# Value-matrix rows of 272 columns, 288 floats apart, with six zero router columns; two tiles of x loaded later

## The reference

```python
# x (4, 1024, 256), ctx (4, 77, 256), side (4, 16), 16 heads of 64
q = LN2(LN(x)) @ Wq;  k, v = split(LN1(ctx) @ Wkv)
q = q * (1 + side) + side                        # per batch and head
attn = softmax(q @ k.T * 64 ** -0.5)             # per head, over 77 rows
x = x + concat_heads(attn @ v) @ Wout
# experts on y = LN(x)
logits = y @ Wr                                  # 9 experts
w, idx = top_k(softmax(logits), 2);  w = w / w.sum()
x = x + sum_e w_e * ((silu(y @ Wg[e]) * (y @ Wu[e])) @ Wd[e])   # 256 -> 704 -> 256
```

## Time and profile before

| | us |
|---|---|
| median of 3 runs (lowest, highest) | 809.7 (808.88, 810.03) |
| profiled execution, its own time | 810.75 |
| its span, first to last instruction | 809.0 |
| TensorE busy | 781.2 |
| VectorE busy | 662.2 |
| ScalarE busy | 622.3 |
| GpSimd busy | 386.2 |

### The profile page before, as it was taken

How to read it: one execution, slowest core, us unless ns; L and a number is a source line. 1 busy time by engine, 2 the same in 40 slices (tenths; PEclk the granted TensorE clock), 3 DMA queues, 4 the chain that set the end, 5 groups by cost and what they waited for, 6 DMA issues and landing times.

```text
span 809.0 us, 19727 instructions
## 1 busy us (share of the span) xinstructions
PE 781.2 (97%) x6011; PEld 744.7 (92%) x6011; DVE 662.2 (82%) x1614; ACT 622.3 (77%) x1967; POOL 386.2 (48%) x539
## 2 busy tenths in 40 slices
PE   7998999999999999998999999999999999999994
PEld 7766999999999999897999999999999999999994
DVE  7787798898888887888688988788887878879782
ACT  5878898899899888844677877777787877778772
POOL 3321587688678766771324343332434333233343
PEclk9999999999999999998999999999999999999998
DMA  8375710410410020635475373465656556483222
GB/s 278 116 187 163 224 35 34 144 41 27 148 38 28 34 86 28 212 115 172 102 216 141 51 218 87 104 151 141 182 151 163 146 144 164 90 224 79 47 26 28
DMA packets 78212, 96.40 MB, mean 119 GB/s; under 512 B 10723, under 2 KB 65435, under 8 KB 77979
## 3 DMA queue, kind: packets, MB, share of 16 engines
q1 hardware_dynamic: 64667, 77.25, 31.2%
q0 software_dynamic: 13440, 17.90, 12.6%
HBM read 109.45 MB, written 30.23 MB: 173 GB/s over the span
## 4 chain that ended last, share of the span: by engine, by line
PE 88%; DVE 4%; ACT 2%; issue 2%; POOL 1%; DVEq 1%; DMA 0%; SPq 0%; POOLq 0%; ACTq 0%
PE banks L355 25%; PE banks L356 25%; PE banks L357 25%; PE banks L1471 4%; PE banks L1637 2%; PE banks L1451 2%; PE banks L1485 2%; DVEq L1690 1%; PE banks L1422 1%; PE banks L1434 1%; ACT wq_head L1071 1%; PE banks L1355 1%; ACT prob L1138 1%; PE banks L1609 0%; DVE hid_f L2128 0%
## 5 line engine op out<-in xcount | busy, mean ns | idle before, releaser
L355 PE MATMUL banks<-tok_t_hi,wgt_hi 128*128 128x256 f32 x704 | 201.5, 286 | 3.7 <-issue 2.8
L1015 POOL DMA_INDIRECT result<-res,tok_id x72 | 123.9, 1721 | 164.1 <-ACT res L1273 144.7
L357 PE MATMUL banks<-tok_t_hi,wgt_lo 128*128 128x256 f32 x704 | 197.1, 280 | 0.0
L356 PE MATMUL banks<-tok_t_lo,wgt_hi 128*128 128x256 f32 x704 | 197.0, 280 | 0.0
L1138 ACT ACTIVATE prob<-banks,row_min 128x77 f32<-128x77 f32 x512 | 161.5, 374 | 2.3 <-DVE row_min L1840 2.3
L355 PEld LDWEIGHTS banks<-tok_t_hi,wgt_hi 128*128 128x128 f32 x704 | 133.6, 190 | 5.9 <-issue 5.8
L356 PEld LDWEIGHTS banks<-tok_t_lo,wgt_hi 128*128 128x128 f32 x704 | 133.2, 189 | 0.0
L357 PEld LDWEIGHTS banks<-tok_t_hi,wgt_lo 128*128 128x128 f32 x704 | 133.1, 189 | 0.0
L1138 ACT ACTIVATION_READ_ACCUMULATOR prob<-banks,row_min 128x1 f32 x512 | 130.6, 257 | 0.0
L355 PE MATMUL banks<-wgt_hi,hid_hi 128*128 128x256 f32 x360 | 101.2, 281 | 0.7 <-DVE hid_hi L2156 0.7
L356 PE MATMUL banks<-wgt_lo,hid_hi 128*128 128x256 f32 x360 | 100.8, 280 | 0.0
(11 more groups left out here) (273 smaller groups left out, 2208.6 us busy)
## 6 DMA issues: line engine op xcount, KB each, us to landing
wgt<-in_L_ffn_Wg SPq DMA_DIRECT2D x29, 704.0 KB
wgt<-in_L_ffn_Wu SPq DMA_DIRECT2D x29, 640.0 KB
wgt<-in_L_ffn_Wd SPq DMA_DIRECT2D x29, 640.0 KB
tok<-expert_in SPq DMA_DIRECT2D x32, 258.0 KB, 3.8
spare_wgt<-in_L_ffn_Wg SPq DMA_DIRECT2D x9, 704.0 KB, 4.5
spare_wgt<-in_L_ffn_Wu SPq DMA_DIRECT2D x9, 640.0 KB, 6.1
spare_wgt<-in_L_ffn_Wd SPq DMA_DIRECT2D x9, 640.0 KB, 5.7
valmat_f<-valmat_dram SPq DMA_DIRECT2D x4, 1197.0 KB, 6.3
```

Of the source, the lines that this page charges most:

```text
L355: nc.tensor.matmul(to, a[0], b[0], start=first, stop=False)
L356: nc.tensor.matmul(to, a[0], b[1], start=False, stop=False)
L357: return nc.tensor.matmul(to, a[1], b[0], start=False, stop=last)
L1015: nc.gpsimd.indirect_dma_start(out, bass.IndirectOffsetOnAxis(ap=tok_id[:, t % NOTES, a:a + 1], axis=0), res[i][:, a, :], None, compute_op ...
```

## The change

A value row has DE = 272 columns, the next multiple of 16 after 266; in the SBUF tiles of the values a row takes VAL_ROW = 288 floats, of which 272 are used. The router matrix in `wr_sb` has VX = 16 columns a part, seven of them zero (one was zero before), so Wout's router columns and everything made of them carry six more zeros. The columns of the keys stay 10 (`EX`). `wout_sb` grows with DE, and the early part of x ends at tile 11 instead of 13; tiles 12 to 15 come with the third load. A tile `line_gap` of 16 floats lies ahead of the values, and `x_odd` is gone: `x_variance` uses the columns of `x_off`, which `x_offset` writes later.

In the built program the places in a line of 128 bytes are now: `prob_t` 96, `valmat_hi` and `valmat_lo` 32 with every row (1,152 bytes apart), `zn_t` 96, `keymat_hi` 96, `keymat_lo` 32, `tok_t` 32, `hid` 32, all expert weights 96.

```diff
+LINE = 32
+HALF_LINE = LINE // 2
 HKE = HK + EX
-DE = D + EX
+DE = -(-(D + EX) // HALF_LINE) * HALF_LINE
+VX = DE - D
+VAL_ROW = -(-DE // LINE) * LINE
...
-X_PARTS = [(0, TB), (TB, TB + 6), (TB + 6, 2 * TB), (2 * TB, 3 * TB), (3 * TB, T)]
+X_PARTS = [(0, TB), (TB, TB + 4), (TB + 4, 2 * TB), (2 * TB, 3 * TB), (3 * TB, T)]
...
-        wr_sb = sb("wr_sb", [P, KT, EX])
+        wr_sb = sb("wr_sb", [P, KT, VX])
...
-        x_odd = sb("x_odd", [P, T], F32, att)
...
+        sb("line_gap", [P, HALF_LINE], F32, att)
         whole = ExitStack()
-        late_f = sb("late_f", [P, 2, KC, DE], F32, whole)
+        late_f = sb("late_f", [P, 2, KC, VAL_ROW], F32, whole)
         whole.close()
-        valmat_hi = sb("valmat_hi", [P, 2, KC, DE], F32R, att)
+        valmat_hi = sb("valmat_hi", [P, 2, KC, VAL_ROW], F32R, att)
...
-            return vals[0:P if c1 < KC else KLAST, b % 2, c0:c1, :]
+            return vals[0:P if c1 < KC else KLAST, b % 2, c0:c1, 0:DE]
...
-                sp.dma_start(valmat_f[:, b % 2, 0:KC - 1, :],
+                sp.dma_start(valmat_f[:, b % 2, 0:KC - 1, 0:DE],
...
-                mean, odd, var = (z[:, own] for z in (x_mean, x_odd, x_var))
+                mean, odd, var = (z[:, own] for z in (x_mean, x_off, x_var))
...
-                    nc.tensor.matmul(to[:, c * EX:(c + 1) * EX], wout_t[:, k, c * P:(c + 1) * P], wr_sb[:, k, :],
+                    nc.tensor.matmul(to[:, c * VX:(c + 1) * VX], wout_t[:, k, c * P:(c + 1) * P], wr_sb[:, k, :],
...
-                                 [v[0:n, half, m, :] for v in (valmat_hi, valmat_lo)], m == 0, m == KC - 1)
+                                 [v[0:n, half, m, 0:DE] for v in (valmat_hi, valmat_lo)], m == 0, m == KC - 1)
```

More of the change, by code:

```diff
@@ L637, in load_valmat @@
                 rows = valmat_dram[b].rearrange("h k n -> (h k) n")
-                sp.dma_start(valmat_f[:, b % 2, 0:KC - 1, :],
+                sp.dma_start(valmat_f[:, b % 2, 0:KC - 1, 0:DE],
                              rows[0:(KC - 1) * P].rearrange("(c p) n -> p c n", p=P)).then_inc(valmat_loaded, 16)
-                sp.dma_start(valmat_f[0:KLAST, b % 2, KC - 1, :], rows[(KC - 1) * P:]).then_inc(valmat_loaded, 16)
+                sp.dma_start(valmat_f[0:KLAST, b % 2, KC - 1, 0:DE], rows[(KC - 1) * P:]).then_inc(valmat_loaded, 16)
             load_valmat(0)
@@ L1092, in round_router @@
                     ins = nc.scalar.activation(keymat[0][:, :, k * HKE + HK:(k + 1) * HKE],
-                                               wr_sb[:, k, :].unsqueeze(1).to_broadcast([P, B, EX]), ACT.Copy)
+                                               wr_sb[:, k, 0:EX].unsqueeze(1).to_broadcast([P, B, EX]), ACT.Copy)
                 ins.then_inc(wr_cols_hi, 1)
@@ L1401, in _ @@
                 for k in range(KT):
-                    nc.tensor.matmul(to[:, c * EX:(c + 1) * EX], wout_t[:, k, c * P:(c + 1) * P], wr_sb[:, k, :],
+                    nc.tensor.matmul(to[:, c * VX:(c + 1) * VX], wout_t[:, k, c * P:(c + 1) * P], wr_sb[:, k, :],
                                      start=k == 0, stop=k == KT - 1)
             for k in range(KT):
-                mm = nc.tensor.matmul(to[:, PAIRS * EX:(PAIRS + 1) * EX], ones[:], wr_sb[:, k, :], start=k == 0, stop=k == KT - 1)
+                mm = nc.tensor.matmul(to[:, PAIRS * VX:PAIRS * VX + EX], ones[:], wr_sb[:, k, 0:EX], start=k == 0, stop=k == KT - 1)
             mm.then_inc(router_made, 1)
@@ L1795, in _ @@
                         hi, lo = (z[:, :, k * HKE + HK:(k + 1) * HKE] for z in keymat)
-                        ins = nc.vector.tensor_tensor(lo, wr_sb[:, k, :].unsqueeze(1).to_broadcast([P, B, EX]), hi.bitcast(F32),
+                        ins = nc.vector.tensor_tensor(lo, wr_sb[:, k, 0:EX].unsqueeze(1).to_broadcast([P, B, EX]), hi.bitcast(F32),
                                                       ALU.subtract)
```

10 lines of the change are left out of this document (5 added, 5 removed).

## The result

| | before | after |
|---|---|---|
| median of 7 runs (lowest, highest), us | 809.44 (808.88, 810.39) | 812.05 (811.53, 813.02) |
| profiled execution | 810.75 | 811.53 |
| its span | 809.0 | 809.8 |
| TensorE busy | 781.2 | 781.3 |
| attention, first product of tile 0 to last of tile 30 | 258.38 | 259.56 |

The account below looks back on a forecast made before the run. TensorE, busy 97% of the span, was taken as the bound. Terms -0.5 + 0.3 + 0.2 + 0 + 0 summed to 0.0 us, so the median stayed at 809.7 us, range 806.4 to 813.4.

Parts of the forecast that it names:

- the price of a step: TensorE products priced from one start to the next: 123.8 ns for 266 columns in attention, mean 116.1 for 256 in experts.
- the two kinds: Expert products of 256 columns run in unbroken series at about 113.4 ns (fast) or 117.9 ns (slow) each.
- (a): The 960 attention products, six columns wider with equally placed rows: -0.5 us, between -3.2 and +1.2.
- by the expert stretch's mean: Attention step priced from the mean of both kinds, 116.1 + 16 x 0.45 = 123.3 ns against 123.8.
- the line of the slow kind: Slow expert products scaled by 0.45 ns a column: about 122.4 ns at 266 columns, 125.1 at 272.
- The rival at full price: Attention: placement gives nothing, six columns cost the slope, 126.5 ns a product; 812.8 us, chance 0.12.
- (b): TensorE products that make the values, six columns wider: +0.3 us, from 0 to 0.6.
- (c): Wider copies, roundings and store on the values' trip through DRAM: together +0.2 us, 0 to 0.5.
- (d): Preparation: two tiles of x load later, their VectorE statistics fit into a wait at the end of step 2: 0.
- (e): Everything behind wr_sb moves 32 bytes, operand distances stay: 0, between -9.0 and +5.9 us in the expert stretch.
- My rival: Moving operands off a 64-byte boundary lose the fast kind in the expert stretch: 815.6 us, 817.3 with attention; chance 0.15.
- The clock: Shifted work near 377 us escapes the half clock or meets another: 806.3 or 813.1 us, chances 0.05 and 0.03.

Follow-up runs that it names:

- x3: The kernel before with only the second half of the split weights (wgt_hi1, wgt_lo1) moved by 128 bytes: 807.31 us in one run.
- r4: The changed kernel's places, rows 288 floats apart, with 266 columns instead of 272: 811.27 us, 1.0012.
- r2: The changed kernel with hid1_lo (and res1 behind it) moved by the 32 bytes that the others were moved: 810.61 us, 1.0010.
- b6: The kernel before with hid1_lo alone moved by 128 bytes: 811.67 us, 1.0014.
- r5: r1 with hid1_lo moved on by 128 bytes as well: 811.41 us, 1.0016.
- b1: The kernel before with hid1_lo alone moved 32 bytes further on: 809.39 us, 1.0001.
- x2: The kernel before with the second half of the split weights and hid1_lo moved by 128 bytes: 808.17 us, 0.9984.
- r3: The changed kernel with attention's and the experts' operands put on multiples of 64 bytes, half-line distance kept: 813.0 us, 1.0036.
- r1: The changed kernel with the expert tiles moved back to multiples of 64 bytes, but not hid1_lo: 812.54 us, 1.0034.

## Why the prediction was wrong, point by point

**What bounds the kernel, the price of a step, the two kinds.** Right in the main, and all that followed rests on it: the stretches of TensorE's products give 2.2 of the 2.6 us. Two things about the kinds were too simple. "A series keeps its kind to its end" holds once a series is fast, but it can begin slow: in x3 the odd series take about 118 ns a step for their first 2 to 10 products and then 113 to 114 to the end, so the fast kind is one that a series falls into. And there are three levels, not two: the slow odd series of before took 118.4 to 119.1 ns, not 117.9.

**(a) Attention.** The failed step is "by the expert stretch's mean". The bounds were sound, +1.2 at the upper end (125.1 ns), and the runs gave exactly that end: 125.17. That it is this end is partly luck, since it is reached by another way than the line of the slow kind: at the same places 266 columns cost 123.47 ns, a nanosecond above that line, and the six columns 0.28 ns each, not 0.45. I carried the mixture of kinds from products of 256 columns to products of 272. No placement tried brings 272 columns clearly below it: 125.17 and 125.19 with distances of 64 and 192 in turn, 125.30 with 64 throughout, 125.94 with 0 and 128 in turn. Term: -0.5 forecast, +1.2 measured. The rival at full price (126.5) was nearer in sum, but not in mechanism, since r4 shows equal starts to be worth 0.43 ns and six columns to cost 1.70 at these places.

The rows say 1.70 ns for six columns at after's places and 3.35 at the best ones. The Trainium skill (TensorE: Matmul & The Clock Gate, section "Wait — 56ns, not 53.3ns?") has N / 2.4 GHz plus 2.5 ns, so 2.5 ns for six columns at any place. That lies between the two; no level here is near its own 115.8.

**(b), (c) The values' way.** Right in sign, and about half the size: from the router products to the last early value product +0.17 us, from the keys to the first attention product +0.09. VectorE's copies after, and the roundings on the chain, answer to the earlier trace rows:

```profile
L1779 DVE COPY late_f<-banks 52x544 f32<-52x544 f32 x4 | 2.8, 711 | 0.1
```

```profile
73.89 2.62 ACT valmat_hi L1150 x4
```

A mean of 695 ns became 711, 2.57 us became 2.62. Together +0.26 against the forecast 0.5.

**(d) Two tiles of x later.** Right. VectorE after, at the end of step 2, to be read with the earlier trace rows:

```profile
81.63 0.41 DVE L1792 TENSOR_TENSOR zn_t_lo<-banks,zn_t_hi 128x256 fp32r<-128x256 f32 x1
81.96 0.74 DVE L1765 BATCH_NORM_STATS2 x_stats<-xs 128x6 f32<-128x256 f32 x2
83.90 0.42 DVE L1826 TENSOR_TENSOR xs<-xs,banks 128x256 f32<-128x256 f32 x1 [1.19 <-PE banks L361]
```

The pair of statistics starts without a wait, so x was there. The wait behind it shrank from 1.80 to 1.19 us and still ends on TensorE.

**(e) The shift.** The failed step is "but all alike: distances between moving and stationary operands stay". It was false for one tile. The kernel's text shows it: `hid1_lo` is created in the `late` block, ahead of `wr_sb`. (It was false in 256 bytes for a second pair: `x_odd` lay between `zn_t` and `keymat`, and without its 128 bytes their distances went from 128 and 64 to 0 and 192. That one cost nothing, the score products' mean step is 193.8 ns in both.) I listed the places of "hid" as one thing and didn't ask which of its four parts lie elsewhere. My rival had the right place and sign but the wrong mechanism (a start off a multiple of 64): r2 leaves every tile off it and has all its series back. Both the prediction and this rival also had the wrong unit, as b6 shows. The sentence that the two kinds "occur after one another at equal addresses" was wrong in the same way. Weights and `hid` each have two copies, at different places in 256 bytes, which a line of 128 doesn't tell apart. Term: 0 forecast, +0.7 us measured in the stretches of the experts (+1.1 by the steps alone), within the bounds of -9.0 and +5.9. That most of it is `hid1_lo` is shown by r2, which takes 0.6 us of it back. The Trainium skill's line of 16 bytes (SBUF — State Buffer, section "Specifications (TRN2)"), which I quoted against this rival, doesn't describe this effect: the runs disagree.

**The clock.** What the rival named (work that shifts by a microsecond escapes part of the half clock) occurred in the profiled execution and gave 0.7 us, not the 3.4 at which it was priced. It is not sure to be scatter. Six of the seven profiled kernels with 272 columns have the short half clock (all but r5), and two of the thirteen with 266 (b1 and x3). The mean granted clock of single executions says the same: it is 0.991 or 0.992 in 18 of 58 with 272 columns, and never above 0.990 in the 232 on record in the experiments with 266. So the change probably brings it about part of the time. By what way isn't shown, and the medians contain it.

**The numbers.** 812.05 lies in the 806.4 to 813.4. The forecast said no change, and 2.6 us, clear of the noise, are slower: it failed because two terms that I had set at their middle, (a), or at zero, (e), both went to the slow side, +1.7 and +0.7 us from where I had them. That the "full price" rival's 812.8 is so near is luck, since it puts 2.6 us on attention alone, which measured 1.2.

## What to carry to other kernels

Before a tile's size is changed, list the places of both operands of every long series of products, copy by copy and part by part, in 256 bytes, and see which distances change; a tile that lives in another block than its siblings is the one that is missed. Count series by kind and by buffer in the timeline, since a mean over all hides a group that went from 6 to 0 and one that could go to 20. A term between two known levels deserves a run at one placement more before its mean is believed.

## What the runs showed of the hardware

A series of down products (256 columns, fp32r) runs at 113.4 ns a product or at 117.7 to 118.8, and how often at which depends on the pair of distances between the stationary parts and the moving weights in 256 bytes: 20 of 20 fast at (64, 192), 0 or 1 of 20 at (192, 192) and (192, 32). Such a series may need up to ten products, and in a few cases more, to reach the fast level. A move of one operand by 128 bytes changes the counts; a move of all by 128 changed some (even down series 15 instead of 8 and 10) but not the mean step. What in the chip does this isn't shown. Gate and up went from 24 to 47 of 64 in x2 and to 8 in r3, and no simple rule in these distances fits all of their counts; the distance between tokens and weights is the same in r1 and r5, which differ only in `hid1_lo` and have 10 and 18.

Attention products of 266 columns take 121.9 to 123.9 ns by their places, those of 272 columns 125.2 to 125.9. A width that is a whole number of half lines brought no advantage, and six more columns cost 1.7 to 3.4 ns.
